# A conditioned layer and an expert layer on one core: the first loads from one queue, cond biases multiplied earlier, the second norm's variance fetched before its centring

## What is computed

```python
# layer 0: a small network makes scale and shift from t
h = silu(noise_encoding(t, 128) @ W1 + b1)         # 16 x 512
h = h @ W2 + b2
scale, shift = h @ Wsc + bsc, h @ Wsh + bsh        # per batch and feature
# _layer_norm: mean and variance over all tokens and features of a batch
out = silu(scale * _layer_norm(x, gamma, beta) + shift) @ W_in + b_in
out = silu(scale * _layer_norm(out, gamma, beta) + shift) @ W_out + b_out
x = out + x
# layer 1: one expert of eight for each batch
h = gelu(x @ Wi[e] + bi[e]);  o = h @ Wo[e] + bo[e]    # 512 -> 2048 -> 512
y = row_norm(o + x) * gamma[e] + beta[e]               # over the features of a token
```

## Time and profile before

| | |
|---|---|
| time, median of 3 runs | 1782.98 us (1782.56 to 1783.33) |
| time of the profiled execution | 1783.88 us |
| span of the profiled execution | 1782.1 us |
| PE busy | 1767.6 us, 99% |
| DVE, ACT, POOL busy | 1286.0, 975.2 and 104.3 us |
| DMA | 189.35 MB, 106 GB/s in the mean |

### The profile page before, as it was taken

How to read it: one execution, slowest core, us unless ns; L and a number is a source line. 1 busy time by engine, 2 the same in 40 slices (tenths; PEclk the granted TensorE clock), 3 DMA queues, 4 the chain that set the end, 5 groups by cost and what they waited for, 6 DMA issues and landing times.

```text
span 1782.1 us, 22261 instructions
## 1 busy us (share of the span) xinstructions
PE 1767.6 (99%) x7936; PEld 1455.0 (82%) x7936; DVE 1286.0 (72%) x2139; ACT 975.2 (55%) x1544; POOL 104.3 (6%) x196
## 2 busy tenths in 40 slices
PE   8999999999999999999999999999999999999998
PEld 5888888888888888888888888888888888888886
DVE  5876777777777677777777677677777767767566
ACT  4656455565545656456564555645556554565442
POOL 1000000000000000000000000000000000000000
PEclk9999999999999999999999999999999999999999
DMA  7232331432323233332332323333133332322321
GB/s 290 74 110 74 122 110 52 138 112 98 109 88 140 75 102 110 117 109 72 122 109 98 109 72 122 111 120 109 59 136 108 98 110 95 133 75 88 117 95 59
DMA packets 39089, 189.35 MB, mean 106 GB/s; under 512 B 7043, under 2 KB 7043, under 8 KB 20548
## 3 DMA queue, kind: packets, MB, share of 16 engines
q1 hardware_dynamic: 36290, 183.42, 28.8%
q0 software_dynamic: 2400, 3.97, 2.2%
q10 hardware_dynamic: 290, 0.55, 0.1%
HBM read 171.10 MB, written 16.81 MB: 105 GB/s over the span
## 4 chain that ended last, share of the span: by engine, by line
PE 98%; DVE 1%; DMA 0%; issue 0%; POOL 0%; ACT 0%; POOLq 0%; ACTq 0%; DVEq 0%
PE hid_ps L494 39%; PE out_acc L494 39%; PE blk_ps L494 18%; DMA x<-in_bias_rows 0%; PE hid_ps L432 0%; PE out_acc L512 0%; PE blk_ps L423 0%; PE out_acc L520 0%; PE out_acc L524 0%; POOL rstd_r L1108 0%; PE out_acc L521 0%; DVE x L853 0%; DVE bn_r L906 0%; DVE r_sb L901 0%; PE hid_ps L512 0%
## 5 line engine op out<-in xcount | busy, mean ns | idle before, releaser
L494 PE MATMUL hid_ps<-x_hi,wi_hi 128*128 128x512 f32 x1024 | 398.7, 389 | 0.1
L494 PE MATMUL hid_ps<-x_lo,wi_hi 128*128 128x512 f32 x1024 | 398.4, 389 | 0.0
L494 PE MATMUL hid_ps<-x_hi,wi_lo 128*128 128x512 f32 x1024 | 398.4, 389 | 0.0
L494 PE MATMUL out_acc<-wo_hi,g_hi 128*128 128x512 f32 x1016 | 395.2, 389 | 0.0
L494 PE MATMUL out_acc<-wo_lo,g_hi 128*128 128x512 f32 x1016 | 395.2, 389 | 0.0
L494 PE MATMUL out_acc<-wo_hi,g_lo 128*128 128x512 f32 x1016 | 395.2, 389 | 0.0
L657 ACT ACTIVATE g_sb<-hid_ps,bi_sb 128x512 f32<-128x512 f32 x256 | 176.0, 688 | 318.6 <-PE hid_ps L494 318.3
L752 DVE TENSOR_TENSOR g_lo<-g_sb,g_hi 128x512 fp32r<-128x512 f32 x254 | 173.8, 684 | 188.5 <-ACT g_hi L661 186.7
L614 ACT ACTIVATE wo_hi<-stage 128x512 fp32r<-128x512 f32 x254 | 160.7, 633 | 173.1 <-PE out_acc L494 173.1
L494 PEld LDWEIGHTS hid_ps<-x_hi,wi_hi 128*128 128x128 f32 x1024 | 192.3, 188 | 41.0 <-DVE x_lo L752 0.8
L494 PEld LDWEIGHTS hid_ps<-x_hi,wi_lo 128*128 128x128 f32 x1024 | 192.2, 188 | 40.0
(11 more groups left out here) (134 smaller groups left out, 1668.0 us busy)
## 6 DMA issues: line engine op xcount, KB each, us to landing
stage<-in_expert_w SPq DMA_DIRECT2D x128, 1024.0 KB, 4.9
x<-in_xT SPq DMA_DIRECT2D x15, 1024.0 KB, 6.1
out_y<-r_sb SPq DMA_DIRECT2D x15, 1024.0 KB, 5.2
rows<-in_expert_rows SPq DMA_DIRECT2D x16, 512.0 KB, 6.6
mv_all<-mv_dram POOLq DMA_DIRECT2D x30, 128.0 KB, 4.1
stage<-in_cond_w SPq DMA_DIRECT2D x4, 512.0 KB, 11.2
affine_sb<-in_affine SPq DMA_DIRECT2D x3, 512.0 KB, 10.9
x<-in_xT SPq DMA_DIRECT2D x2, 512.0 KB, 7.1
```

What stands on the lines that cost most here:

```text
L494: last = pe.matmul(dst, w[wp], xs[xp], start=start and i == 0, stop=stop and i == 2)
```

## The change

Loads: ACT issues none any more. SP issues `head`, W1, x of batch 0 in four chunks of 256 KB, `bias_rows`, both halves of W2, and then goes on as before. W2's halves and gamma and beta are laid out in DRAM so that each load is one block; x of all batches is kept as plain feature rows of 2 KB, so that the load of a later batch reads four such rows for a partition where it read one of 8 KB.

PE: the b2 strips come behind the fillers, which are nine now and follow the first product; the first average comes ahead of W2; the bias strips of scale and shift are a function of their own, called for chunks 0 and 1 between W2's first half and the second average and for 2 and 3 behind the second half; three fillers and not four, six and not seven around `scale_shift(0)`; none between the first half and the first average. Since four more banks are in use at that time, the first results go to the banks of `out_acc`.

DVE: `stats` waits for a chunk of x and not for a half; `first_var(1)` comes ahead of `centre(0, 1, 0)`, and `affine(0, 1, 0)` ahead of `centre(0, 1, 1)`.

```diff
-        stat_bank = [hid_ps[1], blk_ps[1]]
+        stat_bank = [out_acc[0], blk_ps[1]]
+        m1_bank, m2_bank = out_acc[2], out_acc[3]
...
+            load(head_sb[:, :], head, ld_head)
             load(w1_raw, W1, ld_w1)
+            for c in range(DC):
+                load(x_sb[0][:, c, :], xT[0, c * P:(c + 1) * P, :], ld_first[c])
+            load(x_sb[1][0:1, 0:3, :].rearrange("p c n -> p (c n)"), bias_rows, ld_bias)
             for h in range(2):
-                load(half(x_sb[0], h), xT[0, :, h * HALF:(h + 1) * HALF], ld_first[h])
-            load(half(w2_raw, 1), W2[:, HALF:2 * HALF], ld_w2[1])
+                load(half(w2_raw, h), W2[h], ld_w2[h])
...
-                load(x_sb[b % 2][:, :, :].rearrange("p c n -> p (c n)"), xT[b], ld_x[b % 2])
+                load(x_sb[b % 2][:, :, :], xT[b].rearrange("(c p) n -> p c n", p=P), ld_x[b % 2])
...
-            def scale_shift(c):
-
+            def scale_shift_bias(c):
                 bias = bcond_row[:, 2 * P * c:2 * P * (c + 1)]
                 strips(cond_bank[c], ones[:, 0:BLOCK], of_cond(bias), 2 * BLOCK, start=True)
+
+            def scale_shift(c):
+
                 pe.wait_ge(ld_cond[c], 16)
...
-            strips(blk_ps[0], enc_sin[:, :], of_w(w1_raw), P, start=True, stop=True).then_inc(s_mm1, 1)
+            strips(m1_bank, enc_sin[:, :], of_w(w1_raw), P, start=True, stop=True).then_inc(s_mm1, 1)
+            keep_warm(hid_ps[0], 9)
             pe.wait_ge(s_ones, 1)
             pe.wait_ge(ld_bias, 16)
-            strips(blk_ps[1], ones[:, 0:BLOCK], of_w(b2_row), P, start=True)
-            keep_warm(hid_ps[0], 10)
+            strips(m2_bank, ones[:, 0:BLOCK], of_w(b2_row), P, start=True)
+            pe.wait_ge(s_average, 1)
+            pe.wait_ge(s_mv, 1)
+            average_of(0, 0, mv[:, 0, 0:1])
             pe.wait_ge(s_pad, 2)
             pe.wait_ge(s_m1, DC)
             w2_half(0)
-            keep_warm(hid_ps[0], 3)
-            pe.wait_ge(s_average, 1)
-            pe.wait_ge(s_mv, 1)
-            average_of(0, 0, mv[:, 0, 0:1])
-            w2_half(1).then_inc(s_mm2, 1)
+            scale_shift_bias(0)
+            scale_shift_bias(1)
             pe.wait_ge(s_sq, 1)
             average_of(0, 1, dev[:, 0, 1:2])
-            keep_warm(hid_ps[0], 4)
+            w2_half(1).then_inc(s_mm2, 1)
+            scale_shift_bias(2)
+            scale_shift_bias(3)
+            keep_warm(out_acc[1], 3)
             pe.wait_ge(s_m2, 1)
             scale_shift(0)
-            keep_warm(blk_ps[1], 7)
+            keep_warm(out_acc[1], 6)
...
-            act.dma_start(head_sb[:, :], head).then_inc(ld_head, 16)
-            act.dma_start(half(w2_raw, 0), W2[:, 0:HALF]).then_inc(ld_w2[0], 16)
-            act.dma_start(x_sb[1][0:1, 0:3, :].rearrange("p c n -> p (c n)"), bias_rows).then_inc(ld_bias, 16)
...
-                    dve.wait_ge(ld_first[m // 2], 16)
+                    dve.wait_ge(ld_first[m], 16)
...
             first_mean(1)
+            first_var(1)
             centre(0, 1, 0)
-            first_var(1)
+            affine(0, 1, 0)
             centre(0, 1, 1)
-            affine(0, 1, 0)
             affine(0, 1, 1)
```

More of the change, by code:

```diff
@@ L235, in build @@
         ld_cond = [sem(f"ld_cond{m}") for m in range(DC)]
-        ld_first = [sem("ld_first_a"), sem("ld_first_b")]
+        ld_first = [sem(f"ld_first{c}") for c in range(DC)]
         ld_affine = [sem(f"ld_affine{c}") for c in range(DC)]
@@ L328, in load_affine @@
             def load_affine(c):
-                load(affine_sb[:, c].rearrange("p a n -> p (a n)"), affine[c], ld_affine[c])
+                load(affine_sb[:, c], affine[c].rearrange("a p n -> p a n"), ld_affine[c])
             def load_w_in(c):
                 load(w_raw[0][:, c, :], W_in[c * P:(c + 1) * P, :], ld_w_in[c])
+            load(head_sb[:, :], head, ld_head)
             load(w1_raw, W1, ld_w1)
+            for c in range(DC):
+                load(x_sb[0][:, c, :], xT[0, c * P:(c + 1) * P, :], ld_first[c])
+            load(x_sb[1][0:1, 0:3, :].rearrange("p c n -> p (c n)"), bias_rows, ld_bias)
             for h in range(2):
-                load(half(x_sb[0], h), xT[0, :, h * HALF:(h + 1) * HALF], ld_first[h])
-            load(half(w2_raw, 1), W2[:, HALF:2 * HALF], ld_w2[1])
-            load(affine_sb[:, 0, 0, :], affine[0, :, 0:S], ld_affine[0])
+                load(half(w2_raw, h), W2[h], ld_w2[h])
+            load(affine_sb[:, 0, 0, :], affine[0, 0], ld_affine[0])
             load_cond(0)
-            load(affine_sb[:, 0, 1, :], affine[0, :, S:2 * S], ld_beta0)
+            load(affine_sb[:, 0, 1, :], affine[0, 1], ld_beta0)
             load_w_in(0)
@@ L457, in scale_shift, with w2_half @@
                 last.then_inc(s_mmcond, 1)
+            def w2_half(h):
+                pe.wait_ge(ld_w2[h], 16)
+                for k in range(h * (DC // 2), (h + 1) * (DC // 2)):
+                    last = strips(m2_bank, m1[:, k, :], of_w(w2_raw[:, k, :]), P, stop=(k == DC - 1))
+                return last
             pe.wait_ge(s_zero, 1)
@@ L962, in _ @@
             dve.wait_ge(s_mm1, 1)
-            dve.transpose(m1_raw[:, :, :].rearrange("p c r -> p (c r)"), blk_ps[0][:, 0:P]).then_inc(s_m1turn, 1)
+            dve.transpose(m1_raw[:, :, :].rearrange("p c r -> p (c r)"), m1_bank[:, 0:P]).then_inc(s_m1turn, 1)
             for m in range(DC):
@@ L968, in _ @@
             dve.wait_ge(s_mm2, 1)
-            dve.transpose(m2[:, :, :].rearrange("p c r -> p (c r)"), blk_ps[1][:, 0:P]).then_inc(s_m2, 1)
+            dve.transpose(m2[:, :, :].rearrange("p c r -> p (c r)"), m2_bank[:, 0:P]).then_inc(s_m2, 1)
             centre(0, 0, 0)
@@ L1165 @@
     arrays = {
-        "xT": a["x"].transpose(0, 2, 1).reshape(B, DC, P, S).transpose(0, 2, 1, 3).reshape(B, P, DC * S),
+        "xT": a["x"].transpose(0, 2, 1),
         "itok": a["itok_B_0_7"],
@@ L1169 @@
                                [columns(A[n]) for n in ("b1", "b_in", "b_out")], axis=1),
-        "W1": A["W1"], "W2": chunks(A["W2"]),
+        "W1": A["W1"], "W2": A["W2"].reshape(2, DC // 2, P, D).transpose(0, 2, 1, 3).reshape(2, P, DC // 2 * D),
         "cond_w": np.stack([A["Wsc"], A["Wsh"]]).reshape(2, DC, P, DC, P // BLOCK, BLOCK)
@@ L1175 @@
                        .reshape(1, -1),
-        "affine": np.stack([A["gamma"].T, A["beta"].T]).reshape(2, DC, P, S).transpose(1, 2, 0, 3)
-                    .reshape(DC, P, 2 * S),
+        "affine": np.stack([A["gamma"].T, A["beta"].T]).reshape(2, DC, P, S).transpose(1, 0, 2, 3),
         "W_in": A["W_in"], "W_out": chunks(A["W_out"]),
```

1 line of the change is left out of this document (removed).

## The result

The changed kernel takes 1778.64 us in the median of 20 runs (1778.03 to 1780.9), the kernel before 1783.33 us (1782.16 to 1784.75, 20 runs). The ratio is 0.9977, with a 95% interval from 0.997 to 0.9983: 4.7 us by the medians, where 4.3 were predicted. The profiled execution took 1778.37 us with a span of 1776.6, which is 5.5 us less than the span of before. Of the 20 times of the changed kernel, 14 lie between 1778.0 and 1779.6 and six between 1780.0 and 1780.9.

What follows compares the result with a forecast made beforehand. PE, busy without a wait from 48 us on, bounds the kernel, so only a shorter start wins. Front 3.3, chunk loop 0.7 and second norm 0.3 make 4.3 us: from 1782.98 to 1778.7 us, range 1777.3 to 1781.0.

Steps and rivals of the forecast that it cites:

- PE waits for nothing in the long part, so only the start counts: From 48 us to the end: PE runs without a wait, so whatever it reaches earlier at 42 us is subtracted whole.
- The head stays first: Start of the loads: the angle encoding and PE's first product at 5.54 us don't move; W1 goes out 0.45 us later.
- Front, 3.3 us: Start on PE: DVE's turn of scale_shift(0)'s result at 14.8 instead of 18.11 us, gain 3.3 us, bounds 2.3 and 4.2.
- From the first average to scale_shift(0), 3.4 us: Front on PE: W2 halves, cond biases, second average and three fillers take 3.4 us, so scale_shift(0) starts at 14.1 us.
- Fillers set the first average: Front on PE: nine fillers end at 10.2 us, after the average's input at 9.6; first average taken at 10.7 us.
- Chunk loop: Scale and shift for chunks 1 to 3: 0.24 us off each loop, 0.7 us in all, at least 0.3; loads cost nothing.
- Their landings stay: Loads behind W2's first half: issued some 2.2 us later, but standing in a backlog, so they land when they did before.
- The third rival: Chunk loop: loads become the limit from 2.3 us of lateness on; gain only 2 to 3.5 us, 1780.2 us; chance 0.05.
- Second norm, 0.3 us: Second norm on DVE: affine(0) starts at 39.45 instead of 39.79 us, gain 0.3 us, bounds 0 and 0.5.
- Rival 1: Front: clock rises after 12 us, strips between averages run slow; gain 3.3 us or less, 1779.7 to 1781; chance 0.17.
- Rival 2: Front loads: x quarters land one after the other, 2.9 us each; gain 0.7 us, 1782.3 us; chance 0.04.
- Rival 5: Long part: x loads in 2 KB rows hold SP's queue and the weight pairs; slower, 1786.6 us or more; chance 0.04.

Runs made afterwards that it cites:

- the one with the late head: Head load issued by ACT instead of SP, beside W1 from SP, the rest as in the changed kernel; median 1779.97 us, 1.3 above the changed kernel.

## Why the prediction was right, and where it wasn't

The median fell into the range and 0.1 us beside the value, and that close hit is luck in part. The profiles show the start 5.50 us shorter (53.24 to 47.74 us): 4.93 for the front and 3 x 0.24 for the bias strips, less 0.36 for a load, and 0.21 for the second norm, where 3.3, 0.7 and 0.3 were predicted. A front that won 1.6 us too much stood against a loop that won 0.3 too little and against the 0.8 us that the medians show less than the profiles. The kernel that the prediction describes, the one with the late head, wins 4.26 us by its profile, almost to the sum, but 3.4 by its median (1783.36 to 1779.97).

- **PE waits for nothing in the long part, so only the start counts**: right, to 0.1 us in every profile (1728.9 us).
- **"The head stays first, so [...] the first product of PE at 5.54 us don't move"**: this step failed. It moved to 4.61 us, as head landed 1.6 us behind its issue and not 2.6. DVE's statistics started at 5.57 instead of 6.57. I had bounded the average's input by that transpose, so my bound of 9.8 us for the first average was passed as well: 8.98. (The sum there, 6.57 + 2.62 + 0.26, is 9.45 and not 9.6 us; the forecast doesn't hang on it.)
- **Front, 3.3 us**: 4.93 in the profile. With head moved back it is 3.3 (14.81 instead of 18.11 us), so the sum behind it was right and the missing term is the one above, with 1 us of it direct and 0.6 by the pace of the fillers.
- **From the first average to scale_shift(0), 3.4 us**: 3.49.
- **Fillers set the first average**: of the kernels with nine fillers whose profiles are here, only in the one with the late head. In the changed one they keep the clock, and x's last quarter sets the average; its landing, 7.8 us, was right (7.9).
- **Chunk loop, 0.7 us, loads "Nothing"**: each distance 0.24 us shorter, as said, but 0.36 us were given back to the load of gamma and beta of chunk 2, 0.4 in all instead of 0.7. I had taken W_in as the one to watch, and took the landings behind W2 as unchanged; this one came at 19.1 us instead of 18.4 (7.50 + 10.9), and W_in of chunk 2 at 21.1 (9.88 + 11.2) instead of 20.4. "Their landings stay" is the step that failed. The third rival, which I gave 0.05, was there in small from the start, since the front won more.
- **Second norm, 0.3 us**: 0.32 at affine(0), 0.2 at the start of the long part. The late h_lo of chunk 3, "Nothing, with 0.2 us left", probably costs the 0.1 us between.
- **Rival 1 (the clock)**: the size is right, the mechanism in part. In the execution of the upper group that was profiled, what costs 2.5 us isn't a late rise but a fall behind idle time, which the prediction doesn't have. The mean granted clock points to the same in three of the six times above 1780 us and not in the other three, where a late rise, the rival's own mechanism, stays open.
- **Rival 2 (quarters one after the other)**: false; they landed 3.5 to 4.7 us behind their issues, all four on their way at once. **Rival 5 (x loads in the long part)**: 7.3 instead of 6.1 us to land, none of it seen.

## What to carry to other kernels

A small load that the first computation needs is best issued first, ahead of the large ones: here 15.5 KB issued 0.46 us ahead of 256 KB in one queue let the first product start 1 us sooner than issued from a second queue at the same time, and that was worth 1.3 us of the median, more than the second norm's reordering. Fillers that keep TensorE's clock must be judged by what they cover: too many are the path, too few cost more through the strips behind them; look at the granted clock of the stretch after the wait, in more than one execution. When a start phase gets shorter, list every load of the next phase by its landing time, since one of them is the next limit.

## What the runs showed of the hardware

The granted clock is shown as 1.00 in the first microseconds of every profile here, where 512 columns take 0.43 us, which is 1.2 GHz; it goes to 0.50 only when the clock falls later on. The pace, not that column, tells the level at the start. A rise at 6 us instead of 13 doesn't last by itself: in three profiles with TensorE idle for 1.4 to 2.3 us in one piece ahead of the first average it stood at 0.50 from 12 to 16 us. A fourth, with 0.6 and 0.8 us in two pieces, ran three fillers in 1.65 us as well; with 1.0 and 0.3 us (the kernel with the bias strips back) and with one piece of 0.6 (the profile after) the clock stayed. The early rise alone doesn't bring the fall: the second of the two more profiles of the changed kernel had the same fast fillers (2.34 us for nine), idled 0.62 us and kept its clock. How much idle time it takes isn't shown, since no run varied that alone.
